# Query projected straight into its turned form in a fused gated-linear-attention and expert block

## The reference, cut to what matters

```
h = layernorm(x) * (1 + ca) + sa
q, k, v = h @ Wq, h @ Wk, h @ Wv            # [4096, 256] each, 16 heads of 16
gate = exp(log_sigmoid(h @ Wgk1 @ Wgk2 + bgk2) / 16)
for t: state = state * gate[t] + v[t] k[t]^T;  out[t] = state q[t]
x = x + ga * ((layernorm(out) * gamma + beta) * silu(h @ Wg)) @ Wout
h = layernorm(x) * (1 + cb) + sb
x = x + gb * (sum over the top 2 of 8 experts of w_e * (gelu(h @ W1_e + b1_e) @ W2_e + b2_e))
```

## Time and profile before

| | |
|---|---|
| median of 3 runs | 968.58 us (968.27 to 972.14) |
| the profiled execution | 966.65 us |
| its span | 964.6 us |
| TensorE matmul busy | 834.3 us, 86% of the span |
| VectorE busy | 660.1 us, 68% |
| ScalarE busy | 440.1 us, 46% |

### The profile page before, as it was taken

How to read it: one execution, slowest core, us unless ns; L and a number is a source line. 1 busy time by engine, 2 the same in 40 slices (tenths; PEclk the granted TensorE clock), 3 DMA queues, 4 the chain that set the end, 5 groups by cost and what they waited for, 6 DMA issues and landing times.

```text
span 964.6 us, 23092 instructions
## 1 busy us (share of the span) xinstructions
PE 834.3 (86%) x6879; PEld 731.7 (76%) x6880; DVE 660.1 (68%) x1527; ACT 440.1 (46%) x1164; POOL 382.5 (40%) x404
## 2 busy tenths in 40 slices
PE   4798889988888889888239989998998998999992
PEld 4576666666666666666139989898998998999992
DVE  2468888888888888887536757667476574765751
ACT  1476666666666666664124333233333333333330
POOL 5124444444444344443212343434433443354442
PEclk9999999999999999998559999999999999999997
DMA  6401111111111111111223242424225233222222
GB/s 233 157 18 57 51 50 56 40 55 56 44 56 46 49 56 50 50 50 41 89 91 106 47 119 55 122 45 126 45 45 131 45 100 76 45 46 46 46 24 31
DMA packets 53191, 65.01 MB, mean 67 GB/s; under 512 B 5955, under 2 KB 48661, under 8 KB 53013
## 3 DMA queue, kind: packets, MB, share of 16 engines
q1 hardware_dynamic: 29908, 36.00, 11.4%
q0 software_dynamic: 13440, 18.36, 10.5%
q10 hardware_dynamic: 9792, 10.03, 3.9%
HBM read 39.47 MB, written 24.90 MB: 67 GB/s over the span
## 4 chain that ended last, share of the span: by engine, by line
PE 45%; DVE 27%; issue 14%; DMA 9%; DVEq 2%; SPq 1%; ACT 1%; ACTq 0%; POOL 0%; POOLq 0%
PE p_a L1117 20%; PE p_cum L1117 8%; PE p_gz L1117 5%; DVE w_hi L895 5%; PE p_qk L1117 4%; DMA ln_host<-expert_rows 4%; DMA out_dram<-host_n,tok 4%; PE p_v L1117 4%; DVE w_parts L918 2%; PE p_a L1287 1%; DVE st L827 1%; DVE x L946 1%; PE p_qk L1136 1%; DVE host_o L907 1%; DVE st_x L827 1%
## 5 line engine op out<-in xcount | busy, mean ns | idle before, releaser
L648 POOL DMA_INDIRECT out_dram<-host_n,tok x72 | 150.6, 2092 | 267.7 <-DMA out_dram<-host_n,tok 195.6
L1117 PE MATMUL p_a<-w_hi_r,acts_r 128*128 x1152 | 207.7, 279 | 0.1
L1117 PEld LDWEIGHTS p_a<-w_hi_r,acts_r 128*128 128x128 f32 x1152 | 178.1, 188 | 0.3 <-issue 0.3
L1117 PE MATMUL p_a<-w_lo_r,acts_r 128*128 x576 | 160.8, 279 | 0.0
L789 ACT ACTIVATE x_host<-p_a,mods 128x256 f32<-128x256 f32 x72 | 36.8, 561 | 191.2 <-PE p_a L1287 189.6
L1117 PEld LDWEIGHTS p_a<-w_lo_r,acts_r 128*128 128x128 f32 x576 | 108.2, 188 | 0.0
L1079 DVE CAST acts_r<-acts 128x2048 fp32r<-128x2048 f32 x36 | 44.2, 1227 | 81.2 <-ACT acts L780 81.2
L600 POOL TENSOR_TENSOR ln_host<-w_parts,gam 128x256 f32<-128x256 f32 x32 | 23.1, 722 | 188.5 <-DVE w_parts L936 188.5
L625 POOL DMA_INDIRECT expert_rows<-rows,pos x64 | 64.1, 1002 | 49.4 <-issue 32.4
L1081 DVE TENSOR_TENSOR acts_r<-acts,acts_r 128x2048 fp32r<-128x2048 f32 x36 | 82.5, 2293 | 1.2
L895 DVE TENSOR_TENSOR w_hi<-p_a,upto 128x1024 f32<-128x1024 f32 x64 | 75.3, 1218 | 3.1 <-PE p_a L1117 2.9
(11 more groups left out here) (210 smaller groups left out, 1828.7 us busy)
## 6 DMA issues: line engine op xcount, KB each, us to landing
w<-in_L_ffn_W_dram SPq DMA_DIRECT2D x16, 1024.0 KB, 8.2
ln_host<-expert_rows ACTq DMA_DIRECT2D x36, 272.0 KB, 3.0
host_x<-in_L_attn_x_dram SPq DMA_DIRECT2D x64, 128.0 KB, 2.1
out_dram<-x SPq DMA_DIRECT2D x32, 128.0 KB, 1.7
expert_rows<-pad_rows SPq DMA_DIRECT2D x16, 136.0 KB, 1.7
acts<-in_L_wmod_dram SPq DMA_DIRECT2D x1, 1536.0 KB, 6.5
out_dram<-host_n,tok POOLq DMA_INDIRECT x72, 4.7
b_all<-in_L_ffn_b_dram SPq DMA_DIRECT2D x1, 1024.0 KB, 7.8
```

The costliest lines, as they stand in the source:

```text
L648: nc.gpsimd.indirect_dma_start(out=out, out_offset=bass.IndirectOffsetOnAxis(ap=tok[u][:, h:h + 1], axis=0), in_=y_out[u][:, h, :], in_off ...
L1117: return nc.tensor.matmul(dst, lhsT, rhs, start=start, stop=stop, skip_group_check=True)
```

## The change

Only k is projected by rows, as six products of 256 moving columns. q is projected in turned form: the weights are the stationary operand and the turned input moves, so each product has 128 moving columns, and there are two blocks of 128 outputs with six products each, twelve in all. They write `p_qk[:, 0:256]`, where the turned q stood before, and the signal `proj_ready` now comes from the last of them. ScalarE's copy L723 takes 256 columns in place of 512, and two transposes of four remain. Nothing else is different: every wait stands where it stood.

```diff
@@ -189,7 +189,7 @@
-        qk = [in_w2.take(2 * D) for i in range(2)]
+        qk = [in_w2.take(D) for i in range(2)]
@@ -720,7 +720,7 @@
                     act_e.wait_ge(proj_ready, f + 1)
                     after(act_e, u_ready, f - 1)
-                    A.copy(qk[v][:], p_qk[:]).then_inc(qk_taken, 1)
+                    A.copy(qk[v], p_qk[:, D:2 * D]).then_inc(qk_taken, 1)
@@ -1212,7 +1212,15 @@
                     project(p_v[:, 0:D], wv_hi_r, wv_r)
                     after(pe, h2T_ready, s - 1)
-                    project(p_qk[:], wqk_hi_r, wqk_r).then_inc(proj_ready, 1)
+                    project(p_qk[:, D:2 * D], wqk_hi_r[:, :, D:2 * D], wqk_r[:, :, D:2 * D])
+                    for blk in range(KD):
+                        cols = slice(blk * P, (blk + 1) * P)
+                        n = 0
+                        for w, h in ((wqk_hi_r, hT_hi_r), (wqk_r, hT_hi_r), (wqk_hi_r, hT_lo_r)):
+                            for j in range(KD):
+                                last = mm(p_qk[:, cols], w[:, j, cols], h[:, j, :], n == 0, n == 3 * KD - 1)
+                                n += 1
+                    last.then_inc(proj_ready, 1)
@@ -1235,7 +1243,7 @@
                     pe.wait_ge(qk_taken, f + 1)
-                    transposes(p_qk, qk[v], 2 * KD, qkT_ready)
+                    transposes(p_qk[:, D:2 * D], qk[v], KD, qkT_ready)
@@ -1251,7 +1259,7 @@
-                        last = mm(p_u[:, j * P:(j + 1) * P], qk[u][:, D + j * P:D + (j + 1) * P],
+                        last = mm(p_u[:, j * P:(j + 1) * P], qk[u][:, j * P:(j + 1) * P],
                                   vn[u][:, j * QUADS:(j + 1) * QUADS], True, True)
```

## The result

The changed kernel takes 973.66 us (median of 20 runs, 969.56 to 979.34). Beside it the kernel before took 970.24 (20 runs, 967.88 to 972.96). The ratio is 1.0032, with a 95% interval of 1.0018 to 1.0047. By the bound of the forecast (0.5%) that is no change. It is not nothing, though: the interval leaves 1 out, and some 3 us were added. The forecast had +0.5 us. The mean granted clock over the 20 runs of the changed kernel is 0.949 (0.940 to 0.953).

A forecast was written before the change was run, and what follows sets the result against it. A VectorE chain with one excursion through TensorE was taken to bound each step, hiding nearly all growth. The profiled 966.65 plus about 0.5 gave 967.2; the runs' median lies 1.93 higher, so 969 us, range 966 to 1008.

The forecast's parts named there:

- the likeliest case: Whole kernel: no measurable change, the growth being almost all hidden; between 966 and 973 us, chance 0.55.
- the slow products: Rival at q's twelve products: rounded products are slow when narrow, 0.2175 us each, giving 1005 us; chance 0.30.
- What bounds the kernel: A step's length is a VectorE chain with one 1.5 us excursion through TensorE; TensorE work ahead of `p_cum` is free up to its earliness.
- The price of a narrow product: q's projection on TensorE: each 128-column rounded product takes 0.117 us, twelve take 1.40 us.
- The rivals with 0.14 and 0.2175: q's products dearer: 0.14 to 0.16 us each, 975 to 983 us, chance 0.10; or 0.2175, 1005 us, chance 0.30.
- Growth and earliness: Ahead of `p_cum`: 0.70 us more a step against TensorE's idle 0.68 and 0.90 us, leaving 0.02 us a loop turn.
- First and last projection: Ahead of `p_cum`: the first projection, idle 0.74 us, hides the growth; the last, idle 0.46, is late by 0.24.
- ScalarE: Behind the later `proj_ready`: L723 takes about 0.38 us, L727 and L731 move by about 0.1 us, all hidden, no gain.
- Two transposes less ... Nothing comes of it: TensorE behind `p_cum` and expert scores: 0.24 us saved gains nothing, since y already has 0.40 us to spare before L946.
- the forecast's own sum: Time added over the whole kernel: 15 x 0.02 + 0.24, about 0.5 us.
- Theory C: Experiments' theory: the gap from missing transposes lets TensorE's clock fall; whole-kernel fills expected at ratio 0.998 to 1.001 and 0.999 to 1.0015.

The follow-up runs named there:

- chunks alone: Either kernel with the expert stage left out, so only the 32 chunks, routing and tables remain: before 491.96 us, changed 494.97 us.
- each fill: Changed kernel with k's two transposes made twice, or with three identity transposes behind the ranks: 971.56 or 971.06 us; without the expert stage 492.38 or 492.39.

## Why the prediction was right, and which step of it failed

The range held, but in part by luck: 973.66 lies just above the 973 up to which the likeliest case alone was to reach, and the range went further only for the slow products, which did not come. Of the 4.66 us above the forecast of 969, 1.66 are the kernel before itself, whose median is 970.24 over 20 runs and was 968.58 over three.

**What bounds the kernel: right.** The chain runs on VectorE with the excursion through TensorE. Three runs show it from three sides: extra work ahead of `p_cum` is free, more than the earliness is paid in full, and a shorter excursion shortens each step.

**The price of a narrow product: right, a little high.** I took 0.117 us; it is (228.98 - 227.69) / 12 = 0.1075. The rivals with 0.14 and 0.2175 fall. The Trainium skill's rule for a weight load ("TensorE: Matmul & The Clock Gate", section "LDWEIGHTS") gives an estimate of 107 ns for 128 columns, which was for q the better price; k's products, with 256 columns, took 0.117 as forecast, where it would have had 0.107 too.

**Growth and earliness: right.** The growth is 1.99 - 1.40 = 0.59 where I had 0.70. Of the idle 0.68 and 0.90 us, 0.09 and 0.31 should be left. The row at 242.37 has 0.27, and in the other step the load runs without a wait laid to L918 (3.0 us in 11 times: every other step). VectorE's wait ahead of L925 stayed at 1.10 us, 24.2 in 22 times.

**First and last projection: half.** At the end I had a lateness of 0.24; VectorE's last wait of this kind, ahead of L925, grew from 1.57 to 1.69 us, by 0.12. The first one I had as hidden. At the full clock it is: in the changed version, chunks alone, VectorE's gates end at 34.97 us and the load starts at 35.03. In the profiled run of the whole changed kernel, at a granted clock of 0.68 from 30 to 37 us, they end at 35.99 and the load starts at 36.55, half a microsecond late. That low stretch at the start is not an effect of the change. It comes in some executions of either version, as here without experts, first before, then after:

```profile
24.00:34.00 10.00, 6.44 (x15) 4.27 (x16) 4.72 (x11) 0.86 (x2) 0.00 (x0) 0.50 1.04 372
...
24.00:34.00 10.00, 7.17 (x26) 5.05 (x27) 4.02 (x10) 1.62 (x3) 0.00 (x0) 1.00 0.98 348
```

**ScalarE: right.** The copy L723 takes 0.37 us (0.38 forecast), and L736 still waits for `p_cum` (0.23 us, 0.21 before), so what was queued there cost nothing.

**"Two transposes less ... Nothing comes of it": this step failed.** For y it was right: y is done at 231.85, and L946 starts at 232.47 with no wait. (In two of the first steps, which do only part of the work, the transposes did give time back: 0.22 us each, 11.01 to 10.79 and 11.87 to 11.65 us from L918 to L918.) But I asked only who waits for the transposes, not what TensorE does with the time that they leave. It stands idle: 0.76 in place of 0.54 us ahead of the next chunk's transposes, 17.4 in place of 12.4 us from 100 to 400. In some executions the granted clock falls to 0.50 right behind that place, and a fall costs 1.4 to 1.6 us on the path. The profiled run of the changed kernel happened to have none in the loop.

Among the full steps nothing else was seen to cost time. In ten of the profiles (all but those with q made twice or the scores moved) the full steps from 125 us on, to the last but one, take 13.12 and 13.39 us by turns within 0.03, with the change or without it; only the two with a fall are longer, 14.84 us each from score to score. At 1.44 us a fall, the 3.3 us would be some 2.3 falls an execution. That is an estimate: no run shows the count, since the one changed version that was profiled with a fall has a single one and is the fastest of its five runs. Nor do the mean clocks of the chunks alone count falls. The profiled run of the version before has 0.953 with no fall among the full steps, that of the changed version 0.957 with one, because the low stretch at the start was in the first and not in the second; and five runs go from 0.949 to 0.966 before, from 0.943 to 0.957 after. In the whole kernel, with more runs, the difference is clear: 0.949 over 20 runs of the changed kernel, 0.954 over 51 of the kernel before and over the 12 of each fill.

That the gap brings the falls rests on this: of the four profiled kernels with the idle piece of 0.76 us three have a fall among the full steps, one of them without narrow products; of the nine whose piece is 0.54 us or shorter none has, both fills with and without experts among them; and in the chunks alone the two fills take back 2.8 and 2.9 us of the mean. What is left there, 0.4 to 0.5 us, is the size of the forecast's own sum.

The Trainium skill describes something of this kind in "TensorE: Matmul & The Clock Gate", section "A second HAM failure mode: psum-queue depth-cycling": short, frequent idling between groups of products lets the clock swing between its two levels. The trace agrees, with pieces of 0.76 and 0.36 us ahead of the fall.

**What stays open.** In the whole kernel, the two fills still stand at 1.0018 (1.0004 to 1.0031) and 1.0026 (1.0011 to 1.004), some 1.7 and 2.5 us over the kernel before, though their mean clock is that of before, 0.954. Both missed what Theory C expected, so the clock does not account for all of the 3 us there. Half a microsecond of it may be the forecast's, at the first and last projection. The remaining 1 to 2 us no run explains, and the intervals of the fills overlap that of the changed kernel (1.0018 to 1.0047): that the fill helps is clear for the chunks alone, as far as different chips can be compared (the kernel before differs by 1.05 us of 970 between them), and only likely for the whole. Likewise, chunks alone with two transposes less lost 2.0 us, and the changed version lost 3.3; half a microsecond of the difference may be the growth at the first and last projection, and the rest is within the scatter of five runs.

## What to carry to other kernels

Work put ahead of a wait is free up to the earliness of the waiting engine, and that can be read to a tenth of a microsecond from the idle time of the weight loads; price new products by the nearest row of the same type, and by the load rather than the columns where they are narrow. Work taken off an engine that is not waited for is not always worth nothing: ask how long TensorE then stands idle, and compare mean granted clocks over many runs (20 told here, five did not), since one profile may miss the falls. Where two engines alternate on the path, look at the order behind the wait before you look at the amount of work: eight columns of scores moved ahead of a wait gave 2%, where the change, with twelve products a chunk more and two transposes less, cost 0.3%.

## What the runs showed of the hardware that was not expected

Rounded float32 products with a new stationary block each follow one another at 0.1075 us with 128 moving columns and at 0.117 with 256: half the columns save a tenth.

The granted clock fell to one half in the middle of a loop in which TensorE is busy nine tenths of the time, behind no longer idle piece than 0.76 us. It was seen in three profiles, all of kernels with two transposes less: the changed one and the one without narrow products, both chunks alone, and the one with q made twice. The profiled run of the whole changed kernel has the same piece and no fall. The nine kernels whose piece was 0.54 us or shorter did not show one among the full steps, in one profile each. A fall lengthened the step by 1.44 us in the first two and by 1.6 in the third.

Adding useless transposes to the changed kernel made its chunks 2.8 us faster in the mean of five runs, on another chip.
